# Attention and experts on one core: VectorE's row-sum work placed one piece to each gap, keys, scale and output projection placed later

## The chip, the core and the metric

The kernel runs on one core of one Trainium2 chip. The metric is device time in microseconds (us), the median of several executions; lower is better. The engines of the core work side by side and wait for one another through semaphores: TensorE (PE, with its weight loads as PEld) does matrix products, VectorE (DVE) and ScalarE (ACT) work on rows of SBUF and PSUM, GpSimd (POOL) adds here, and SyncE (SP) issues the copies.

## What is computed

A transformer block over 2048 tokens of width 128: layer norm, attention of 16 heads of width 64, layer norm, 8 experts (top 2) and a shared one. The attention, cut from the reference, is what the change touches:

```python
xq = xq.reshape(bsz, N_HEADS, seqlen, HEAD_DIM)   # a head takes 128 tokens: 2048 positions of 64
scores = jnp.einsum('bhid,bhjd->bhij', xq, xk) * SCALE
scores = jax.nn.softmax(scores, axis=-1)
out = jnp.einsum('bhij,bhjd->bhid', scores, xv)
out = out.reshape(bsz, seqlen, N_HEADS * HEAD_DIM)
return jnp.einsum('bso,ho->bsh', out, wo)
```

Each head has 2048 queries and 2048 keys; the softmax needs a maximum and a sum for each query.

## The kernel before

**Units and places.** The attention is 32 units of work, numbered 0 to 31: a head and one half of its queries each. Even units do the first half, odd ones the second. Each unit has 32 places, four to a step: at the first two TensorE computes the scores of two key tiles kt (`scores`, L1377), at the other two it weighs the values with the probabilities of the two tiles of the step before (`weigh`, L1410). After a place come the side jobs that a table hands to it (`side_jobs`, L83, from the tables at L41 to L53). Every engine runs through the same places and does its own part of each job, in that order and never out of it. A job moved to another place therefore moves on each engine that has a part in it.

**Pairs of maxima.** At each odd place stands a pair: TensorE multiplies a block of queries of a later unit with two banks of keys (`pair`, L1333, matmul at L1348) into the same two PSUM banks each time. An even pair is reduced by VectorE straight from PSUM (L1108). Of the odd ones all but pair 15 are copied out by ScalarE (`take_pair`, L894), and VectorE reduces the copy after the next odd place (`taken`, L1122); there is one copy buffer. The next pair of TensorE waits until the banks are free, so a late reduction holds up TensorE, and a late `taken` holds up ScalarE's next copy and with it the pair behind. Pair 4 stands at place 1, pair 15 at place 23, pairs 0 to 3 (of the unit after the next) at 25 to 31. After pair 15 VectorE folds the maxima together (L1112) and turns them (`peakT`, L1117).

**Shifts.** SyncE sends `peakT` on as the shifts of the next unit's scores, with eight small copies (`send_shift`, L756, issues at L764, placed at 26). TensorE's first tile of the next unit ends with a product that waits until all eight have landed (L1406).

**Keys of the next head**, in even units alone: for each of two parts TensorE projects keys (L1325); ScalarE casts them (`k_hi`) and copies them (`k_raw`); VectorE takes a difference (`step_k`, L1091); ScalarE rounds it (`round_step`, `d_hi`, L881); VectorE takes what is left (`low_k`, `d_lo`, L1099), which also frees the one bank that all projections share. SyncE then copies the halves of `k_hi`, `d_hi` and `d_lo` across (`swap_hi` L783, `swap_d` L787, issues at L780): two issues each.

**Row sums.** GpSimd adds up the probabilities in two accumulators. In the next unit VectorE turns each (`turn_sum`, L1140, a transpose of 128x1024), reduces it (`add_sum`, L1145), folds and inverts the parts (`fold_sums`, L1153). SyncE spreads the inverse to all rows through DRAM (`spread_sums`, L766), and VectorE scales the unit's output with it (`scale_unit`, L1166). In odd units from unit 3 on TensorE projects the output of the head before (`project`, L1435) and VectorE adds it to the tokens (`add_head`, L1173).

**Queue of SyncE.** SyncE is one queue: an issue that waits for a semaphore holds up all that is placed behind it.

Of the kernel before, what the change touches and what calls it, by code (L numbers as in the profile page):

```python
# [17 lines left out]
HALF = POSITIONS // 2  # L18
BANK = 512
# [19 lines left out]


LONG_JOBS = (  # L41
    {2: ("q", 0), 14: ("k", 0), 18: ("k", 1)},
    {2: ("q", 1), 6: ("v", 0), 14: ("out", 0), 19: ("v", 1)},
)
SEND_PLACE = 26

LOW_PLACES = (
    {3: ("low q", 0), 15: ("step k", 0), 16: ("low k", 0), 19: ("step k", 1), 20: ("low k", 1)},
    {3: ("low q", 1)},
)  # L50
INVERSES = 4
SUM_PLACES = {4: ("turn sum", 0), 6: ("add sum", 0), 8: ("turn sum", 1), 10: ("add sum", 1), 12: ("fold", 0)}
SCALE_PLACE, LATE_SCALE_PLACE = 20, 28  # L53

COUNTED = ("q", "k", "v")
JOBS_PER_HEAD = 6
# [26 lines left out]
def side_jobs(half, sums=True, outs=True, project=True, pairs=True, early=True, last_head=False, before_last=False):  # L83
# [21 lines left out]
    if sums:  # L105
        for place, job in SUM_PLACES.items():
            places[place].append(job)
# [10 lines left out]
def build(nc, x, wq, wk, wv, wo, gate_w, w1, w2, w3, sw1, sw2, sw3, expert_bias, cond, wmod, out):  # L118
    with ExitStack() as ctx:
        def sb(name, shape, dt=F32):  # L120
            return ctx.enter_context(nc.sbuf_tensor(name, shape, dt))

        def sem(name):
            return ctx.enter_context(nc.semaphore(name))
# [32 lines left out]
        acc = sb("acc", [P, 2, HALF])  # L157
        acc_odd = sb("acc_odd", [P, 2, HALF])
# [70 lines left out]
        added = sem("added")  # L229

        part_inverted = sem("part_inverted")
        sums_turned, sums_added, sums_inverted = sem("sums_turned"), sem("sums_added"), sem("sums_inverted")
# [33 lines left out]
        ADDS = TILES - 2  # L266
# [783 lines left out]
        def _(dve):  # L1050
# [86 lines left out]
                dve.wait_ge(o_copied, unit_done)  # L1137
                dve.tensor_tensor(oT[:, half_done, :], o_raw[:, :], job.ps, ALU.mult).then_inc(job_free, 1)

            def turn_sum(unit_done, half_done, odd):  # L1140

                dve.wait_ge(added, unit_done * ADDS + (ADDS - 1 + odd))
                dve.transpose(SumParts(unit_done).turned[odd], (acc_odd if odd else acc)[:, half_done, :]).then_inc(sums_turned, 1)

            def add_sum(unit_done, odd):  # L1145

                parts = SumParts(unit_done)
                dve.wait_ge(sums_turned, unit_done * 2 + (odd + 1))
                dve.tensor_reduce(sum_parts[:, odd * 32:odd * 32 + 32],
                                  parts.turned[odd].rearrange("p (j r) -> p j r", r=32), AX.X,  # L1150
                                  ALU.add).then_inc(sums_added, 1)
# [48 lines left out]
            def body(t):  # L1200
                local = 0
                for p, half, head, unit, plan in units(t):
                    for places in plan:
                        for jobs in places:
                            for kind, i in jobs:
# [14 lines left out]
                                if kind == "turn sum":  # L1220
                                    turn_sum(unit - 1, 1 - half, i)
                                if kind == "add sum":
                                    add_sum(unit - 1, i)
# [319 lines left out]
```

## Time and profile before

| | before |
|---|---|
| median of 3 runs (range) | 1331.19 us (1330.78 to 1331.48) |
| the profiled execution: its own time | 1330.52 us |
| its span, first to last instruction | 1328.6 us |
| granted TensorE clock, mean | 0.994 |
| busy share of the span | PE 96%, DVE 75%, ACT 67%, POOL 84% |

The share of an engine says how long it had an instruction in hand, not how long the program waited for it. TensorE's matmul ends are modelled, so that a stalled matmul can look busy: how TensorE gets on is better read from when its instructions start. A timeline row begins with its start and its length in us; a bracket at its end tells how long the engine sat idle before it and who ended that.

### The profile page before, as it was taken

How to read it: one execution, taken by the hardware profiler on the slowest of the kernel's cores; microseconds unless marked ns; L12 is line 12 of the kernel's file. 1: busy time of each engine (PE TensorE's matmuls, PEld its weight loads, DVE VectorE, ACT ScalarE, POOL GpSimd, SP SyncE). 2: the span in 40 equal slices, each digit the busy share in tenths (PEclk: the TensorE clock that was granted, in tenths of full speed). 3: DMA queues.
4: the chain of work that ended last, by engine and by line, in shares of the span. 5: the costliest groups of instructions: out<-in, count | busy, mean ns of one | idle time of the engine just before them, and what ended most of it. 6: DMA issues, size and time to landing. Idle time of an engine off the chain costs nothing. (4 is left out here: it accounts for less than half of the span.)

```text
span 1328.6 us, 22345 instructions
## 1 busy us (share of the span) xinstructions
PE 1278.2 (96%) x8604; PEld 692.3 (52%) x8604; DVE 994.6 (75%) x1253; ACT 888.4 (67%) x1096; POOL 1115.1 (84%) x507
## 2 busy tenths in 40 slices
PE   7899999999999999999999999999999999998998
PEld 5454454545554454545555454545455544444787
DVE  6677777787777777778777777787877777877575
ACT  6576667676767766676767767676767666774464
POOL 2399899898989899898989898998989898897545
PEclk9899999999999999999999999999999999998999
DMA  7020202020110202020200202020201102001423
GB/s 208 1 48 9 57 9 57 9 57 9 30 28 9 57 9 57 9 56 9 52 14 11 47 9 57 9 56 9 57 10 38 28 2 57 9 10 41 96 72 89
DMA packets 39948, 49.82 MB, mean 37 GB/s; under 512 B 8570, under 2 KB 19202, under 8 KB 39842
## 3 DMA queue, kind: packets, MB, share of 16 engines
q1 hardware_dynamic: 39698, 48.39, 14.4%
q8 instruction: 68, 1.11, 0.4%
q14 instruction: 38, 0.31, 0.1%
q10 hardware_dynamic: 144, 0.00, 0.0%
HBM read 21.83 MB, written 1.24 MB: 17 GB/s over the span
## 5 line engine op out<-in xcount | busy, mean ns | idle before, releaser
L949 ACT ACTIVATE probs<-ps 128x1024 f32<-128x1024 f32 x512 | 499.0, 1032 | 71.0 <-PE ps L1400 64.2
L1418 PE MATMUL ps<-probs,v_sb 128*64 128x512 f32 x2048 | 512.8, 607 | 0.0
L1037 POOL TENSOR_TENSOR acc<-acc,probs 128x1024 f32<-128x1024 f32 x192 | 462.8, 2410 | 49.5 <-ACT probs L949 47.3
L1108 DVE TENSOR_REDUCE peak_parts<-ps 128x2 f32<-128x1024 f32 x297 | 359.0, 1213 | 160.5 <-PE ps L1348 156.6
L1037 POOL TENSOR_TENSOR acc_odd<-acc_odd,probs 128x1024 f32<-128x1024 f32 x192 | 465.1, 2423 | 0.0
L894 ACT COPY peak_copy<-ps 128x1024 f32<-128x1024 f32 x215 | 218.6, 1017 | 257.7 <-PE ps L1348 152.8
L1122 DVE TENSOR_REDUCE peak_parts<-peak_copy 128x2 f32<-128x1024 f32 x215 | 259.9, 1209 | 34.2 <-ACT peak_copy L894 34.2
L1418 PEld LDWEIGHTS ps<-probs,v_sb 128*64 128x64 f32 x2048 | 122.1, 136 | 175.8 <-issue 139.5
L1394 PE MATMUL ps<-q_hi,d_hi 64*128 64x512 f32 x512 | 202.0, 395 | 3.8 <-ACT probs L949 3.8
L1394 PE MATMUL ps<-q_hi,d_swap_hi 64*128 64x512 f32 x512 | 201.8, 394 | 0.4 <-ACT probs L949 0.4
L1400 PE MATMUL ps<-q_hi,d_lo 64*128 64x512 f32 x512 | 201.4, 393 | 0.0
L1400 PE MATMUL ps<-q_hi,d_swap_lo 64*128 64x512 f32 x512 | 201.3, 393 | 0.0
L1397 PE MATMUL ps<-q_lo,d_hi 64*128 64x512 f32 x512 | 200.3, 391 | 0.0
L1397 PE MATMUL ps<-q_lo,d_swap_hi 64*128 64x512 f32 x512 | 200.0, 391 | 0.0
L1348 PE MATMUL ps<-k_swap_hi,q_hi 64*128 64x512 f32 x512 | 119.3, 462 | 19.5 <-DVE peak_parts L1108 14.4
L1031 POOL TENSOR_TENSOR acc_odd<-probs 128x1024 f32<-128x1024 f32 x32 | 76.7, 2397 | 68.8 <-ACT probs L949 68.8
L1348 PE MATMUL ps<-k_hi,q_hi 64*128 64x512 f32 x512 | 121.9, 472 | 11.8 <-DVE peak_parts L1108 7.6
L1348 PEld LDWEIGHTS ps<-k_swap_hi,q_hi 64*128 64x128 f32 x512 | 47.8, 184 | 148.6 <-DVE peak_parts L1108 93.6
L1348 PEld LDWEIGHTS ps<-k_hi,q_hi 64*128 64x128 f32 x512 | 48.1, 184 | 143.0 <-DVE peak_parts L1108 78.1
L1397 PEld LDWEIGHTS ps<-q_lo,d_hi 64*128 64x128 f32 x512 | 94.9, 185 | 13.6
L1394 PEld LDWEIGHTS ps<-q_hi,d_swap_hi 64*128 64x128 f32 x512 | 95.2, 186 | 10.8 <-ACT probs L949 1.3
L1394 PEld LDWEIGHTS ps<-q_hi,d_hi 64*128 64x128 f32 x512 | 95.2, 186 | 10.5 <-ACT probs L949 5.5
(244 smaller groups left out, 1573.3 us busy)
## 6 DMA issues: line engine op xcount, KB each, us to landing
k_swap_hi<-k_hi SPq DMA_DIRECT2D x64, 128.0 KB, 2.5
d_swap_hi<-d_hi SPq DMA_DIRECT2D x64, 128.0 KB, 2.3
d_swap_lo<-d_lo SPq DMA_DIRECT2D x64, 128.0 KB, 2.3
acc_odd<-sums_dram SPq DMA_DIRECT2D x62, 128.0 KB, 2.9
shifts<-peakT SPq DMA_DIRECT2D x256, 0.5 KB
q_hi<-weights_dram SPq DMA_DIRECT2D x8, 256.0 KB, 3.4
q_lo<-weights_dram SPq DMA_DIRECT2D x8, 256.0 KB, 4.9
k_hi<-weights_dram SPq DMA_DIRECT2D x8, 256.0 KB, 6.0
```

Source lines behind the costliest of these rows:

```text
L894: act.copy(peak_copy[:, :, :], ps[:, PEAK_BANK:PEAK_BANK + 2, :]).then_inc(peak_free, 1)
L949: act.activation(probs[:, kt % PROBS, :], ps[:, 2 * place:2 * place + 2, :].rearrange("p a b -> p (a b)"), ACT.Exp, scale=SCALE).then_inc( ...
L1031: pool.tensor_tensor(total, probs[:, kt, :], probs[:, kt + 1, :], ALU.add).then_inc(added, 1)
L1037: pool.tensor_tensor(total, total, probs[:, kt % PROBS, :], ALU.add).then_inc(added, 1)
L1108: dve.tensor_reduce(peak_parts[:, :, i // STRETCHES, i % STRETCHES], ps[:, bank:bank + 2, :], AX.X, ALU.max).then_inc(peak_free, 1)
L1122: dve.tensor_reduce(peak_parts[:, :, i // STRETCHES, i % STRETCHES], peak_copy[:, :, :], AX.X, ALU.max).then_inc(copy_read, 1)
L1348: mm = pe.matmul(ps[:, bank + b, :], q_hi[at, target_parity, q:q + P], keys[at, target_parity, cols], start=True, stop=True, tile_position ...
L1394: pe.matmul(ps[:, slot + b, :], hi[b][at[b], p, cols], q_hi[at[b], p, q], start=kt < 2, stop=False, tile_position=(b * HEAD_DIM, 0), skip_ ...
L1397: pe.matmul(ps[:, slot + b, :], hi[b][at[b], p, cols], q_lo[at[b], p, q], start=False, stop=False, tile_position=(b * HEAD_DIM, 0), skip_g ...
L1400: mm = pe.matmul(ps[:, slot + b, :], lo[b][at[b], p, cols], q_hi[at[b], p, q], start=False, stop=kt >= 2, tile_position=(b * HEAD_DIM, 0), ...
L1418: mm = pe.matmul(ps[at:at + HEAD_DIM, PV_BANK, :], v_sb[:, p, chunk_of(kt) * HEAD_DIM:(chunk_of(kt) + 1) * HEAD_DIM], probs[:, kt % PROBS, ...
```

## The change

In the tables the two parts of the key work go from places 14 and 18 to 18 and 22 (with their steps and lows four places later), the output projection from 14 to 22, the scale from 20 to 27 (28 to 29 in the last unit). The first sum is reduced one place later. The second accumulator is turned in two halves, at places 8 and 10, its reduction goes from 10 to 11, and the fold from 12 to 15.

```diff
 LONG_JOBS = (
-    {2: ("q", 0), 14: ("k", 0), 18: ("k", 1)},
-    {2: ("q", 1), 6: ("v", 0), 14: ("out", 0), 19: ("v", 1)},
+    {2: ("q", 0), 18: ("k", 0), 22: ("k", 1)},
+    {2: ("q", 1), 6: ("v", 0), 19: ("v", 1), 22: ("out", 0)},
 )
 LOW_PLACES = (
-    {3: ("low q", 0), 15: ("step k", 0), 16: ("low k", 0), 19: ("step k", 1), 20: ("low k", 1)},
+    {3: ("low q", 0), 19: ("step k", 0), 20: ("low k", 0), 23: ("step k", 1), 24: ("low k", 1)},
     {3: ("low q", 1)},
 )
-SUM_PLACES = {4: ("turn sum", 0), 6: ("add sum", 0), 8: ("turn sum", 1), 10: ("add sum", 1), 12: ("fold", 0)}
-SCALE_PLACE, LATE_SCALE_PLACE = 20, 28
+SUM_PLACES = {4: ("turn sum", 0), 7: ("add sum", 0), 8: ("turn sum", 1), 10: ("turn sum", 2), 11: ("add sum", 1),
+              15: ("fold", 0)}
+SCALE_PLACE, LATE_SCALE_PLACE = 27, 29
...
-            def turn_sum(unit_done, half_done, odd):
-
-                dve.wait_ge(added, unit_done * ADDS + (ADDS - 1 + odd))
-                dve.transpose(SumParts(unit_done).turned[odd], (acc_odd if odd else acc)[:, half_done, :]).then_inc(sums_turned, 1)
+            def turn_sum(unit_done, half_done, piece):
+
+                dve.wait_ge(added, unit_done * ADDS + (ADDS - 1 if piece == 0 else ADDS))
+                src, to = (acc if piece == 0 else acc_odd)[:, half_done, :], SumParts(unit_done).turned[piece > 0]
+                cols = slice(0, HALF) if piece == 0 else slice((piece - 1) * BANK, piece * BANK)
+                dve.transpose(to[:, cols], src[:, cols]).then_inc(sums_turned, 1)
...
-                dve.wait_ge(sums_turned, unit_done * 2 + (odd + 1))
+                dve.wait_ge(sums_turned, unit_done * 3 + (3 if odd else 1))
```

The new lines push all that stands below them down by up to three lines, so L1348 before is L1351 in the changed kernel.

What the tables do is seen in the engines' order. On VectorE, in the middle of a unit, from the reduction of the first sum (`sum_parts<-k_raw`) on; before:

```order
L1149 TENSOR_REDUCE sum_parts<-k_raw 128x32 [waits sums_turned]
L1143 STREAM_TRANSPOSE acc<-acc_odd 128x1024 [waits added]
L1108 TENSOR_REDUCE peak_parts<-ps 128x2 [waits peak_full]
L1122 TENSOR_REDUCE peak_parts<-peak_copy 128x2 [waits peak_free]
L1149 TENSOR_REDUCE sum_parts<-acc 128x32 [waits sums_turned]
L1157 STREAM_TRANSPOSE acc_odd<-sum_parts 128x64 [waits sums_added]
L1159 TENSOR_REDUCE acc_odd<-acc_odd 32x32 [waits dve_chain]
L1159 TENSOR_REDUCE acc_odd<-acc_odd 32x32 x3
L1163 TENSOR_REDUCE acc_odd<-acc_odd 32x32 [waits dve_chain]
L1164 RECIPROCAL acc_odd<-acc_odd 32x32 [waits dve_chain]
L1108 TENSOR_REDUCE peak_parts<-ps 128x2 [waits peak_full]
L1122 TENSOR_REDUCE peak_parts<-peak_copy 128x2 [waits peak_free]
```

and in the changed kernel:

```order
L1152 TENSOR_REDUCE sum_parts<-k_raw 128x32 [waits sums_turned]
L1146 STREAM_TRANSPOSE acc<-acc_odd 128x512 [waits added]
L1109 TENSOR_REDUCE peak_parts<-ps 128x2 [waits peak_full]
L1123 TENSOR_REDUCE peak_parts<-peak_copy 128x2 [waits peak_free]
L1146 STREAM_TRANSPOSE acc<-acc_odd 128x512 [waits added]
L1152 TENSOR_REDUCE sum_parts<-acc 128x32 [waits sums_turned]
L1109 TENSOR_REDUCE peak_parts<-ps 128x2 [waits peak_full]
L1123 TENSOR_REDUCE peak_parts<-peak_copy 128x2 [waits peak_free]
L1160 STREAM_TRANSPOSE acc_odd<-sum_parts 128x64 [waits sums_added]
```

One half of the transpose now stands behind pair 8 and the copy of pair 7, and the fold, which begins with the 128x64 transpose, behind pair 10 and the copy of pair 9 instead of ahead of them.

On VectorE at the end of an even unit, from the second part of the keys (`ps<-ps,k_raw` is the step, `d_lo` the low) or from pair 14 to pair 0; before:

```order
L1091 TENSOR_TENSOR ps<-ps,k_raw 128x512 [waits raw_ready]
L1099 TENSOR_TENSOR d_lo<-ps,d_hi 128x512 [waits d_hi_ready]
L1170 TENSOR_TENSOR oT<-o_raw,acc_odd 128x512 [waits o_copied,sums_spread]
L1108 TENSOR_REDUCE peak_parts<-ps 128x2 [waits peak_full]
L1122 TENSOR_REDUCE peak_parts<-peak_copy 128x2 [waits peak_free]
L1108 TENSOR_REDUCE peak_parts<-ps 128x2 [waits peak_full]
L1112 TENSOR_REDUCE peak<-peak_parts 128x8 [waits peak_free]
L1117 STREAM_TRANSPOSE peakT<-peak 128x32 [waits shift_ready,peak_ready]
L1108 TENSOR_REDUCE peak_parts<-ps 128x2 [waits peak_ready,peak_full]
```

and in the changed kernel:

```order
L1109 TENSOR_REDUCE peak_parts<-ps 128x2 [waits peak_full]
L1123 TENSOR_REDUCE peak_parts<-peak_copy 128x2 [waits peak_free]
L1109 TENSOR_REDUCE peak_parts<-ps 128x2 [waits peak_full]
L1113 TENSOR_REDUCE peak<-peak_parts 128x8 [waits peak_free]
L1118 STREAM_TRANSPOSE peakT<-peak 128x32 [waits shift_ready,peak_ready]
L1092 TENSOR_TENSOR ps<-ps,k_raw 128x512 [waits raw_ready]
L1100 TENSOR_TENSOR d_lo<-ps,d_hi 128x512 [waits d_hi_ready]
L1109 TENSOR_REDUCE peak_parts<-ps 128x2 [waits peak_ready,peak_full]
L1173 TENSOR_TENSOR oT<-o_raw,acc_odd 128x512 [waits o_copied,sums_spread]
```

The step and the low of the second part of the keys, which stood ahead of pair 14, now stand behind the turning of the maxima and ahead of pair 0; the scale stands behind pair 0.

SyncE's order is the same in both kernels. This is its end of an even unit in the changed one:

```order
L781 DMA d_swap_hi<-d_hi 64x512 [waits d_hi_ready]
L781 DMA d_swap_hi<-d_hi 64x512
L781 DMA d_swap_lo<-d_lo 64x512 [waits job_free]
L781 DMA d_swap_lo<-d_lo 64x512
L765 DMA shifts<-peakT 1x4x32 [waits peak_turned]
L765 DMA shifts<-peakT 1x4x32 x7
```

The copies of the second part of the keys stood ahead of the eight shifts before, too; what these copies wait for now comes later on VectorE and ScalarE.

## Rows read from the trace of the kernel before

**Rows 1.** The whole run's waits: who waited for whom; us in total, times, longest.

```profile
ACT peak_copy L894 <- DVE peak_parts L1122: 104.7, 92, 2.4
```

**Rows 2.** Timeline of PE, end of unit 16: pairs 9 to 12, 14 to 2, then shifts.

```profile
648.64 0.50 PE L1348 MATMUL ps<-k_hi,q_hi 64*128 64x512 f32 x2
650.86 0.51 PE L1348 MATMUL ps<-k_swap_hi,q_hi 64*128 64x512 f32 x2 [0.34 <-ACT peak_copy L894]
...
654.03 0.50 PE L1348 MATMUL ps<-k_swap_hi,q_hi 64*128 64x512 f32 x2
...
656.16 0.51 PE L1348 MATMUL ps<-k_hi,q_hi 64*128 64x512 f32 x2 [0.22 <-ACT peak_copy L894]
...
661.07 0.40 PE L1348 MATMUL ps<-k_swap_hi,q_hi 64*128 64x512 f32 x2
...
664.06 0.50 PE L1348 MATMUL ps<-k_swap_hi,q_hi 64*128 64x512 f32 x2 [0.72 <-DVE peak_parts L1108]
666.32 0.50 PE L1348 MATMUL ps<-k_hi,q_hi 64*128 64x512 f32 x2 [0.35 <-DVE peak_parts L1108]
...
668.62 0.50 PE L1348 MATMUL ps<-k_hi,q_hi 64*128 64x512 f32 x2
...
670.34 0.40 PE L1348 MATMUL ps<-k_swap_hi,q_hi 64*128 64x512 f32 x2
...
673.57 0.40 PE L1406 MATMUL ps<-shifts,minus 64*128 64x512 f32 x2
```

**Rows 3.** Timeline of ACT in unit 16: copy of pair 9, a rounding, copy of pair 1.

```profile
649.79 1.02 ACT L894 COPY peak_copy<-ps 128x1024 f32<-128x1024 f32 x1 [1.66 <-DVE peak_parts L1122]
...
660.79 0.59 ACT L881 CAST d_hi<-ps 128x512 fp32r<-128x512 f32 x1
...
669.16 1.02 ACT L894 COPY peak_copy<-ps 128x1024 f32<-128x1024 f32 x1 [1.90 <-PE ps L1348]
```

**Rows 4.** Timeline of DVE in unit 16: transposes, second key part, pair 15 to pair 0.

```profile
646.23 1.23 DVE L1143 STREAM_TRANSPOSE acc<-acc_odd 128x1024 f32<-128x1024 f32 x1
...
650.86 0.25 DVE L1157 STREAM_TRANSPOSE acc_odd<-sum_parts 128x64 f32<-128x64 f32 x1
...
659.70 0.70 DVE L1091 TENSOR_TENSOR ps<-ps,k_raw 128x512 f32<-128x512 f32 x1
661.42 0.69 DVE L1099 TENSOR_TENSOR d_lo<-ps,d_hi 128x512 fp32r<-128x512 f32 x1 [1.02 <-ACT d_hi L881]
...
665.05 1.21 DVE L1108 TENSOR_REDUCE peak_parts<-ps 128x2 f32<-128x1024 f32 x1
...
666.52 0.21 DVE L1117 STREAM_TRANSPOSE peakT<-peak 128x32 f32<-128x32 f32 x1
666.86 1.23 DVE L1108 TENSOR_REDUCE peak_parts<-ps 128x2 f32<-128x1024 f32 x1
```

**Rows 5.** Timeline of SP, end of unit 16: issues of the second key part and shifts.

```profile
661.41 1.10 SPq L780 DMA_DIRECT2D d_swap_hi<-d_hi  x2
662.55 1.24 SPq L780 DMA_DIRECT2D d_swap_lo<-d_lo  x2
666.76 5.01 SPq L764 DMA_DIRECT2D shifts<-peakT  x8
```

**Rows 6.** Timeline of SP ahead of unit 0: issues of the first shifts.

```profile
42.76 5.01 SPq L764 DMA_DIRECT2D shifts<-peakT  x8
```

**Rows 7.** Timeline of PE, start of unit 0: the product that waits for these.

```profile
48.81 0.80 PE L1406 MATMUL ps<-shifts,minus 64*128 64x512 f32 x2 [1.77 <-DMA shifts<-peakT]
```

**Rows 8.** Timeline of PE, pairs with waits: unit 0, two of unit 29, unit 30.

```profile
77.62 0.50 PE L1348 MATMUL ps<-k_hi,q_hi 64*128 64x512 f32 x2 [0.38 <-DVE peak_parts L1108]
...
1144.72 0.50 PE L1348 MATMUL ps<-k_swap_hi,q_hi 64*128 64x512 f32 x2 [1.43 <-DVE peak_parts L1108]
...
1148.15 0.50 PE L1348 MATMUL ps<-k_hi,q_hi 64*128 64x512 f32 x2 [1.54 <-DVE peak_parts L1108]
...
1172.12 0.51 PE L1348 MATMUL ps<-k_swap_hi,q_hi 64*128 64x512 f32 x2 [0.72 <-DVE peak_parts L1108]
```

## The prediction

> **What bounds the kernel now.** TensorE has the most work, so I ask first what holds it up. The list of the run's waits names ScalarE's copies of pairs, which waited 104.7 us in all for VectorE to reduce the copy before [rows 1]. What that costs TensorE is read from starts, since its ends are modelled: in the timeline of unit 16 I take the distance from one pair to the next, and compare distances that hold the same work. From pair 1 to pair 2 (two score tiles, nothing late) it is 670.34 - 668.62 = 1.72 us. From pair 9 to pair 10, the same work, it is 2.22, and from pair 11 to pair 12 it is 2.13: 0.50 and 0.41 lost, both with ScalarE's copy named in the bracket [rows 2]. ScalarE's own row says why: the copy of pair 9 waited for VectorE's `taken` [rows 3], and that stood behind the first sum and a whole transpose. From pair 0 to pair 1 (two weighings) it is 2.30, from pair 14 to pair 15, the same work, 2.99: 0.69 lost to VectorE [rows 2], where the low of the second key part and the scale stand ahead of pair 14's reduction. Pair 0 comes 2.26 behind pair 15 where 1.72 would do: 0.54 more.
>
> The other thing to see is what must be done when a unit ends. The turned maxima are ready at 666.52 + 0.21 = 666.73 [rows 4], SyncE begins to send the shifts at 666.76 [rows 5], and TensorE uses them at 673.57 [rows 2], 6.81 after the first issue. What the sending needs is seen once, ahead of unit 0, where TensorE really waited for it: from the first issue at 42.76 [rows 6] to the product at 48.81 [rows 7] it is 6.05. So unit 16 has 0.76 us to spare, and no more.
>
> **The change part by part.** All figures are for an ordinary even unit, of which there are 14 (2 to 28).
>
> *Row sums, one piece to a gap.* A whole transpose takes 1.23 and one of 64 columns 0.25 [rows 4], which makes some 0.18 plus 1.02 ns a column: a half is about 0.71 (an estimate), two halves 1.43, 0.2 more than the whole. It buys that 0.5 less stands ahead of the `taken` on which pair 9's copy waits, where 0.50 were lost, and that the whole fold stands behind the `taken` on which pair 11's copy waits, where 0.41 were lost. The dear bound for a half is the whole 1.23: then the first `taken` gains nothing. The cheap one is half of 1.23. I take 0.71, nearest to the two rows that it is drawn from. The copies would then end just as TensorE wants the banks.
>
> *Second key part, and scale, away from pair 14.* The 0.69 goes. Also the reduction of pair 15 began 665.05 - 664.06 = 0.99 after its product [rows 2, 4], since VectorE was still busy; a free engine begins 669.16 - 668.62 = 0.54 after [rows 2, 3]. That is 0.45 more. In all the turned maxima come 0.50 + 0.41 + 0.69 + 0.45 = 2.05 sooner in the unit; I take 2.0, with 1.14 (only the last two) and 2.4 (the short delays of a pair after each wait as well) as bounds.
>
> *What stands behind the turned maxima now.* Step and low of the second key part come after them on VectorE, and SyncE has the copies of that part ahead of the shifts. This is the part that I think decides. The next instruction on VectorE began 666.86 - 666.73 = 0.13 after the turning, a step takes 0.70 [rows 4], I give 0.05 to the hand-over, the rounding on ScalarE takes 0.59 [rows 3], SyncE took it up 661.41 - 661.38 = 0.03 later [rows 3, 5], the four issues ran from 661.41 to 663.79, which is 2.38 [rows 5], and 0.05 go by before the next. Together 3.93 from turned maxima to the first shift issue, where it was 0.03: 3.90 later. The low (0.69) ends inside the first two issues and adds nothing. Bounds: 3.7 without the small gaps; 4.1 if the four issues keep the pace of the last two (1.24 each two, with gaps).
>
> So the shifts are 3.90 - 2.0 = 1.9 later in the unit than before, 0.76 of that was to spare, and the next unit begins **1.14 us** later.
>
> By the Trainium skill, page "DMA: Bandwidth & Descriptors", section "Anatomy of one DMA — SWDGE (gpsimd) path", a copy has a fixed cost of about 2.0 us, most of it the receipt after the last byte. These copies are issued by SyncE, not GpSimd; eight issues in 5.01 put the last one 4.38 after the first, so [rows 6, 7] leave 1.67 for it. By the page's figure an even unit would lose 0.33 more, some 5 us in the run; the measured pair of rows is taken.
>
> *A new wait inside the unit that costs nothing more.* Pair 0's reduction now stands behind step, rounding and low: 0.13 + 0.70 + 0.05 + 0.59 + 0.03 + 0.69 = 2.19 after the turned maxima, ending 3.42 after. TensorE wants to issue pair 1 some 666.32 + 2.30 - 666.73 = 1.89 after them [rows 2], so it waits 1.5 there. ScalarE's exponentials of two tiles also stand behind that rounding. But the end of the unit is set by the shifts, later still, so this wait lies inside the 1.14.
>
> *Moves at no cost.* The first key part goes through the same four places of spacing as the second did. The scale waits for nothing new and lies in the time in which VectorE waits for pair 2; without that cover it would cost its second or less to pair 2. The output projection is the same TensorE work eight places later in odd units; VectorE's addition now waits for it between pairs 14 and 15, but pair 15's product is issued behind the projection anyway. SyncE's eight shifts there have no key copies ahead, and keep their slack. I put odd units at 0, give or take 0.1.
>
> *The units that differ.* Unit 0 has no row sums, and its only VectorE wait of note is 0.38 at pair 0 [rows 8]: it loses 3.90 - 0.45 - 0.76 = 2.7. Unit 29 carries the statistics of the second layer norm in the same gaps as the scale, and TensorE waited 1.43 and 1.54 there [rows 8]; with scale and projection moved I let 2.7 of that go. Unit 30 has no keys: its wait of 0.72 [rows 8] goes, and with the copies' share I take 1.0. Unit 31, the start and the experts: 0.
>
> **Sum.** 14 x 1.14 = 16.0, + 2.7 - 2.7 - 1.0 = 15.0 us. The profiled execution took 1330.5, which gives 1345.5; the median of the runs stands 0.7 above it, so **1346 us**.
>
> **Rivals.**
> *Shifts are not the end of the unit (faster).* If SyncE's send came early enough, TensorE would keep its gains: 0.50 + 0.41 + 0.69 and the 0.54 at pair 0, less the new 1.5 at pair 1, that is -0.6 in 14 units, +1.1 in unit 0, -3.7 in units 29 and 30: 11 less, 1320 us. It decides at 0.76 + 2.0 = 2.8 us: if less than that lies between the turned maxima and the first shift issue. My chain has 3.93, and its largest piece, four issues on one queue, is read directly; for this rival over a quarter of it would have to overlap. By the Trainium skill, the same page and section, waits for semaphores are taken by the issuing sequencer before dispatch, which leaves no room for the shifts to pass the key copies; that SyncE's issues never overlap in these rows agrees. Chance 0.11.
> *Gain and delay cancel.* If the gaps give 2.4 and the chain takes 3.7, an even unit loses 0.54, the run 14 x 0.54 - 1.0 = 6.6: 1338. For no change that can be told, a little more would have to go well (1333). Chance of that 0.07.
> *The halves cost like wholes (slower still).* Then pairs 10 and 12 keep their waits, the maxima come only 1.14 sooner and an even unit loses 2.0: 14 x 2.0 - 1.0 = 27, 1359 us. Against it speaks that a small transpose is five times shorter [rows 4]. Chance 0.08.
> The forecast itself, with its bounds, 0.74.
>
> **How the numbers follow.** About 0.2%, 2.7 us, is what a measurement of this kernel can tell from no change. Slower takes the forecast and the last rival, 0.82; the same 0.07; faster 0.11. The range runs from 1334, just below the case in which most goes well, to 1358, just below the last rival; it leaves out the faster rival and the far end of the slower one, under 2 in 10.
>
> **What would show it.** In an even unit of the changed kernel: pair 9 to 10 and 11 to 12 near 1.75, pair 14 to 15 without a wait (and longer by the key projection); the turned maxima 2.0 sooner in the unit; SyncE's first shift issue about 3.9 behind them; a wait at pair 1 for VectorE; and a wait of TensorE at the shift product (L1409 there) of each odd unit for the shifts, 1.0 to 2.0 us long. If that last wait is missing, the forecast is wrong and the first rival holds. If it is there and the pairs 10 and 12 still wait, the third holds.

## The result and the profile after

| | before | after |
|---|---|---|
| median (range) | 1330.99 us (1325.78 to 1331.48, 4 runs) | 1366.22 us (1363.61 to 1378.64, 4 runs) |
| ratio, 95% interval | | 1.0292 [1.0225, 1.036] |
| profiled execution, span | 1330.52, 1328.6 us | 1378.64, 1376.6 us |
| granted TensorE clock, mean | 0.994 | 0.985 |

Slower, as forecast, but by 35 us where 15 were forecast, and 8 us beyond the range. The four runs of the changed kernel lie 15 us apart. The profiled one, the slowest, has four units with a long stall that is shown below; by the price of one such unit, worked out further down, the other three runs would have had two to three each (an estimate, since they have no trace).

**What came as forecast.** Unit 16 again. TensorE's pairs 9 to 12, 14, 15, 0 to 3 and the first shift product of the next unit, from the timeline of PE after (start and length in us; the bracket is the idle time before and who ended it):

```profile
681.77 0.50 PE L1351 MATMUL ps<-k_hi,q_hi 64*128 64x512 f32 x2
683.52 0.51 PE L1351 MATMUL ps<-k_swap_hi,q_hi 64*128 64x512 f32 x2
685.82 0.50 PE L1351 MATMUL ps<-k_swap_hi,q_hi 64*128 64x512 f32 x2
687.65 0.50 PE L1351 MATMUL ps<-k_hi,q_hi 64*128 64x512 f32 x2
...
692.52 0.42 PE L1351 MATMUL ps<-k_swap_hi,q_hi 64*128 64x512 f32 x2
...
695.61 0.50 PE L1351 MATMUL ps<-k_swap_hi,q_hi 64*128 64x512 f32 x2
697.43 0.50 PE L1351 MATMUL ps<-k_hi,q_hi 64*128 64x512 f32 x2
700.96 0.49 PE L1351 MATMUL ps<-k_hi,q_hi 64*128 64x512 f32 x2 [1.17 <-DVE peak_parts L1109]
702.66 0.41 PE L1351 MATMUL ps<-k_swap_hi,q_hi 64*128 64x512 f32 x2
704.87 0.50 PE L1351 MATMUL ps<-k_swap_hi,q_hi 64*128 64x512 f32 x2
707.68 0.50 PE L1409 MATMUL ps<-shifts,minus 64*128 64x512 f32 x2 [1.61 <-DMA shifts<-peakT]
```

From pair 9 to 10 it is 1.75 now and from 11 to 12 it is 1.83, where [rows 2] had 2.22 and 2.13. Pair 15 and pair 0 come without a wait. Pair 1 waits 1.17 for VectorE, and the shift product waits 1.61 for the shifts. VectorE's half transpose, turning, step, low, pair 0 and scale in the same unit, from its timeline:

```profile
682.28 0.70 DVE L1146 STREAM_TRANSPOSE acc<-acc_odd 128x512 f32<-128x512 f32 x1
...
697.63 0.21 DVE L1118 STREAM_TRANSPOSE peakT<-peak 128x32 f32<-128x32 f32 x1
697.77 0.67 DVE L1092 TENSOR_TENSOR ps<-ps,k_raw 128x512 f32<-128x512 f32 x1
699.08 0.69 DVE L1100 TENSOR_TENSOR d_lo<-ps,d_hi 128x512 fp32r<-128x512 f32 x1 [0.65 <-ACT d_hi L882]
699.69 1.22 DVE L1109 TENSOR_REDUCE peak_parts<-ps 128x2 f32<-128x1024 f32 x1
700.82 2.16 DVE L1173 TENSOR_TENSOR oT<-o_raw,acc_odd 128x512 f32<-128x512 f32 x1
```

and SyncE's queue behind the turning, from the timeline of SP:

```profile
699.08 1.10 SPq L781 DMA_DIRECT2D d_swap_hi<-d_hi  x2
700.22 1.31 SPq L781 DMA_DIRECT2D d_swap_lo<-d_lo  x2
701.58 5.02 SPq L765 DMA_DIRECT2D shifts<-peakT  x8
```

The turned maxima are ready at 697.63 + 0.21 = 697.84, and the first shift leaves at 701.58, 3.74 later (0.03 in [rows 4, 5]). The product comes 6.10 after that, where the prediction took 6.05 from [rows 6, 7]. Unit 16, from shift product to shift product, takes 38.10 (before 37.11). The last row of VectorE's timeline already holds the surprise: the scale takes 2.16.

**What was not forecast.** The waits of TensorE and ScalarE in the whole run (us in total, times, longest), from the list of waits after:

```profile
ACT peak_copy L895 <- DVE peak_parts L1123: 148.5, 107, 7.4
PE ps L1351 <- DVE peak_parts L1109: 43.1, 27, 5.6
PE ps L1409 <- DMA shifts<-peakT: 26.3, 16, 2.6
```

The third row is the forecast wait. The first was 104.7 with a longest of 2.4 [rows 1] and was to shrink; it grew, and 7.4 is a length that nothing in the prediction makes. The group of the scale says where the long ones come from (shortest, median and longest in ns), before

```profile
L1170 DVE TENSOR_TENSOR oT<-o_raw,acc_odd x31: 691/890/2207, 107.7 to 1221.7; 128x512 f32<-128x512 f32 x31
```

and after:

```profile
L1173 DVE TENSOR_TENSOR oT<-o_raw,acc_odd x31: 693/2152/9017, 116.6 to 1269.9; 128x512 f32<-128x512 f32 x31
```

The same instruction on the same data takes up to 9.0 us. Unit 5 is one of four odd units (5, 9, 11, 27) in which it does. VectorE there, timeline after, pair 0 to pair 2:

```profile
265.17 1.23 DVE L1109 TENSOR_REDUCE peak_parts<-ps 128x2 f32<-128x1024 f32 x1
266.31 9.02 DVE L1173 TENSOR_TENSOR oT<-o_raw,acc_odd 128x512 f32<-128x512 f32 x1
275.25 1.21 DVE L1109 TENSOR_REDUCE peak_parts<-ps 128x2 f32<-128x1024 f32 x1
```

GpSimd in the same stretch, the 11th to the 14th add of the unit and the first of the next:

```profile
265.42 2.40 POOL L1038 TENSOR_TENSOR acc<-acc,probs 128x1024 f32<-128x1024 f32 x1
267.74 2.43 POOL L1038 TENSOR_TENSOR acc_odd<-acc_odd,probs 128x1024 f32<-128x1024 f32 x1
270.08 2.40 POOL L1038 TENSOR_TENSOR acc<-acc,probs 128x1024 f32<-128x1024 f32 x1
272.38 2.39 POOL L1038 TENSOR_TENSOR acc_odd<-acc_odd,probs 128x1024 f32<-128x1024 f32 x1
281.87 2.35 POOL L1032 TENSOR_TENSOR acc<-probs 128x1024 f32<-128x1024 f32 x1 [7.09 <-ACT probs L950]
```

TensorE, pairs 2 and 3:

```profile
268.64 0.40 PE L1351 MATMUL ps<-k_swap_hi,q_hi 64*128 64x512 f32 x2
...
276.51 0.79 PE L1351 MATMUL ps<-k_swap_hi,q_hi 64*128 64x512 f32 x2 [5.60 <-DVE peak_parts L1109]
277.11 0.62 PE L1397 MATMUL ps<-q_hi,d_hi 64*128 64x512 f32 x1
```

and each engine's busy time by stretch, with the granted clock in the third column from the right:

```profile
268.00:274.00 6.00, 2.91 (x18) 1.00 (x14) 6.00 (x1) 2.31 (x3) 6.00 (x3) 1.00 0.00 0
274.00:276.00 2.00, 0.00 (x0) 0.00 (x0) 2.00 (x2) 0.00 (x0) 0.77 (x1) 0.80 0.00 0
276.00:282.00 6.00, 5.49 (x24) 3.43 (x26) 3.62 (x4) 3.26 (x4) 0.14 (x1) 0.50 0.01 1
282.00:290.00 8.00, 8.00 (x64) 4.41 (x60) 5.83 (x7) 5.06 (x7) 3.98 (x2) 1.00 0.01 2
```

Read together: the scale began inside the 11th add and ended at 275.33, 0.56 after the 14th had ended (274.77) and GpSimd had nothing ready any more. (In the program the first add of the next unit waits for this scale, `out_scaled`, so only the unit's own adds can go ahead of it.) Four adds ran at their usual 2.4 while it stood. Pair 2's reduction waited behind it, so TensorE sat idle for 5.60, and then went on at the lower of its two clock levels (0.50, which is 1.2 GHz; a score product takes 0.62 instead of 0.39) until 282. Unit 5 took 43.37 where its undisturbed neighbours take 36.85, and the units behind the four took 38.9 to 39.9 instead of 38.0.

### The profile page after: what moved, and what is told of

The parts are those of the page before. It is cut to its first block and busy times, and to the rows that moved or that the text cites. A ratio compares the mean times of both kernels' runs of the same rounds, so it can differ in the third digit from the quotient of the medians.

```text
span 1376.6 us, 22362 instructions
## 1 busy us (share of the span) xinstructions
PE 1289.4 (94%) x8604; PEld 696.2 (51%) x8604; DVE 1059.2 (77%) x1284; ACT 890.5 (65%) x1096; POOL 1113.6 (81%) x507
## 5 line engine op out<-in xcount | busy, mean ns | idle before, releaser
L1038 POOL TENSOR_TENSOR acc_odd<-acc_odd,probs 128x1024 f32<-128x1024 f32 x192 | 470.1, 2448 | 0.0
L895 ACT COPY peak_copy<-ps 128x1024 f32<-128x1024 f32 x215 | 218.5, 1016 | 240.7 <-DVE peak_parts L1123 148.5
L1351 PE MATMUL ps<-k_swap_hi,q_hi 64*128 64x512 f32 x512 | 120.2, 465 | 25.2 <-DVE peak_parts L1109 25.1
L1351 PE MATMUL ps<-k_hi,q_hi 64*128 64x512 f32 x512 | 124.2, 481 | 18.1 <-DVE peak_parts L1109 18.0
L1032 POOL TENSOR_TENSOR acc<-probs 128x1024 f32<-128x1024 f32 x32 | 76.4, 2387 | 62.1 <-ACT probs L950 62.1
L1351 PEld LDWEIGHTS ps<-k_hi,q_hi 64*128 64x128 f32 x512 | 48.4, 186 | 152.4 <-DVE peak_parts L1109 82.2
L1351 PEld LDWEIGHTS ps<-k_swap_hi,q_hi 64*128 64x128 f32 x512 | 48.1, 184 | 151.8 <-DVE peak_parts L1109 92.5
L1403 PEld LDWEIGHTS ps<-q_hi,d_lo 64*128 64x128 f32 x512 | 95.7, 187 | 11.7
```

What stands on the lines that cost most here:

```text
L895: act.copy(peak_copy[:, :, :], ps[:, PEAK_BANK:PEAK_BANK + 2, :]).then_inc(peak_free, 1)
L1032: pool.tensor_tensor(total, probs[:, kt, :], probs[:, kt + 1, :], ALU.add).then_inc(added, 1)
L1038: pool.tensor_tensor(total, total, probs[:, kt % PROBS, :], ALU.add).then_inc(added, 1)
L1351: mm = pe.matmul(ps[:, bank + b, :], q_hi[at, target_parity, q:q + P], keys[at, target_parity, cols], start=True, stop=True, tile_position ...
L1403: mm = pe.matmul(ps[:, slot + b, :], lo[b][at[b], p, cols], q_hi[at[b], p, q], start=False, stop=kt >= 2, tile_position=(b * HEAD_DIM, 0), ...
```

## The experiments

**Is it the scale's place beside GpSimd's adds, and only that?** Theory: VectorE and GpSimd can't both have two operands out of SBUF at once, so VectorE's scale (both operands in SBUF) stands until the adds let it in. Rival: the whole is a matter of the shifts' queue, or of the scale standing at 27 as such. Four kernels. (The letters of theories and rivals here and below are those of the expectations.)

*One operand of the scale from PSUM*, nothing else changed:

```diff
-                dve.tensor_tensor(oT[:, half_done, :], o_raw[:, :], SumParts(unit_done).spread,
+                dve.tensor_tensor(oT[:, half_done, :], o_raw[:, :], ps[:, JOB_BANK, :],
```

> The changed kernel with one operand swapped: the scale multiplies o_raw with a bank of PSUM instead of the spread inverse in SBUF (so the scaling by the row sums is left out; the waits stay). Theory A (a scale with two SBUF operands is kept waiting by GpSimd's adds, from about 2.1 us to 9.0 us, and the 9.0 ones in odd units stop TensorE for 5.6 us and halve its clock for some 7 us): every scale takes about 0.7 us, no odd unit is longer than about 36.9 us, and the run comes to 1345 us plus or minus 4, which is my forecast for the rest. Rival B (the 9 us are a wait of VectorE for something else at that place, a copy of the sums or a semaphore): the long ones stay and the run stays near 1366 or above.

Measured 1347.34 us (1345.87 to 1348.13), ratio to before 1.0138 [1.0116, 1.0159]. The group of the scale in this kernel:

```profile
L1173 DVE TENSOR_TENSOR oT<-o_raw,ps x31: 646/676/686, 116.8 to 1238.6; 128x512 f32<-128x512 f32 x31
```

No scale is longer than 0.69, every one of them beside the same adds; TensorE's wait for the shifts stays (25.6 us, 16 times). So the long scales need the second operand in SBUF, they are worth 1366.2 - 1347.3 = 19 us in the median run, and without them the time is near the forecast of 1346, in part by luck, as is shown below. ScalarE's copies still wait 123.3 us in this kernel (107 times, longest 1.3): of the 148.5 above, the scale made the long ones, and the rest of the growth from 104.7 belongs to the other moves.

*SyncE sends the shifts ahead of the last d copies:*

```diff
-                                    swap_d(head * 2 + (3 + i), Job(jobs_at(t) + (local - 1)), i, 1 - p)
+                                    held = (head * 2 + (3 + i), Job(jobs_at(t) + (local - 1)), i, 1 - p)
+                                    if i == 0:
+                                        swap_d(*held)
...
+                                    if held:
+                                        swap_d(*held)
+                                        held = None
```

> The changed kernel with SyncE's copies of the second key part's d issued behind the eight shifts instead of ahead of them. Theory A (even units end with the shifts, which stand behind those copies): the wait of 1.66 us at the shift product of 15 odd units goes, even units come to about 36.3 us, the run is some 25 us below the changed kernel if the long scales stay as many, so about 1341 us, and the wait at pair 1 stays at 1.2 us. Rival B (even units are held by the wait at pair 1 and the late exponentials, not by the queue of SyncE): the wait moves elsewhere and less than 8 us are won.

Measured 1385.24 us (1375.44 to 1397.82), ratio 1.0406 [1.0334, 1.0478]. The queue did what was meant. SP and TensorE in unit 16 of this kernel, from the timelines (the maxima were turned at 699.07):

```profile
699.10 5.01 SPq L765 DMA_DIRECT2D shifts<-peakT  x8
704.16 1.17 SPq L781 DMA_DIRECT2D d_swap_hi<-d_hi  x2
```

```profile
706.11 0.49 PE L1356 MATMUL ps<-k_swap_hi,q_hi 64*128 64x512 f32 x2
707.14 0.39 PE L1414 MATMUL ps<-shifts,minus 64*128 64x512 f32 x2
```

The wait for the shifts is gone and an undisturbed even unit takes 36.35 instead of 38.0. So the queue costs 1.65 in each even unit, and without it such a unit is shorter than before's 37.11. But eight odd units had a long scale instead of four, and the run came out slower. The two costs have different causes; one was cured, and the other, left to itself, ate the gain.

*Only the scale moved, everything else as before:*

```diff
-SCALE_PLACE, LATE_SCALE_PLACE = 20, 28
+SCALE_PLACE, LATE_SCALE_PLACE = 27, 29
```

> The kernel before with the scale alone moved, from place 20 to 27 (29 in the last unit). Theory A (place 27 is a bad one beside GpSimd's adds): the scale takes 1.4 us or more in most units instead of 0.85 to 1.04, and if it falls into an add as in the changed kernel some odd units lose 6 to 7 us each, with a halved clock behind them; even units gain up to 0.8 us each at pair 15, so 1320 us without any long scale and 1335 to 1360 with some. Rival B (as I had forecast, the scale is free at 27): it takes about 1 us everywhere and the run comes to 1318 to 1324 us.

Measured 1317.66 us (1317.01 to 1318.03), ratio 0.9915 [0.9895, 0.9935]: faster than before. Its scales take 0.88 in odd units and 2.75 in even ones, none more. So place 27 alone isn't the trouble, and moving the scale away from pair 14 is a gain.

*Changed kernel with the keys back at 14 and 18:*

```diff
-    {2: ("q", 0), 18: ("k", 0), 22: ("k", 1)},
+    {2: ("q", 0), 14: ("k", 0), 18: ("k", 1)},
...
-    {3: ("low q", 0), 19: ("step k", 0), 20: ("low k", 0), 23: ("step k", 1), 24: ("low k", 1)},
+    {3: ("low q", 0), 15: ("step k", 0), 16: ("low k", 0), 19: ("step k", 1), 20: ("low k", 1)},
```

> The changed kernel with the keys back at places 14 and 18, their steps and lows at 15, 16, 19 and 20; row sums, scale and output projection stay as changed. Theory A (keys behind the turned maxima cost the even units 1.66 us at the shifts; the scale costs the odd ones): no TensorE wait for shifts and none at pair 1 in even units, which come to about 36 us with a wait near pairs 10 to 13 where fold and first key part now share a gap; long scales may stay. Without them 1318 us, with four of them about 1350. Rival B (the row-sum order itself makes the units longer): even units stay at 37.5 us or more.

Measured 1355.51, 1353.81, 1343.04 and 1313.25 us, four runs of one kernel. In the profiled one (1355.51) five odd units had a long scale and took 43.2 to 43.3; undisturbed even units take 35.95, odd ones 36.75. Five at some 7.8 us each (the price worked out below) are 39 of the 42 us between this run and the fastest, which therefore seems to have had none; it has no trace. So long scales come with the keys at their old places too.

**Does the moment at which the scale meets the add decide?** In the long cases the scale began some 0.9 into the 11th add of the unit, in the harmless odd units of the version with the scale alone 2.03 into the 10th. Two kernels shift only that, with a reduction on VectorE ahead of the odd units' scale whose result nobody reads. In the changed kernel, to get out of that moment:

```diff
+                                if kind == "scale" and half == 1 and unit < UNITS - 1:
+                                    dve.tensor_reduce(sum_parts[:, 0:32], k_raw[:, P:P + 512].rearrange(
+                                        "p (j r) -> p j r", r=16), AX.X, ALU.add)
```

> The changed kernel with one idle reduction of 512 columns (about 0.65 us, result unused) ahead of the scale on VectorE in odd units but the last. In the changed kernel every odd scale begins 0.85 to 0.93 us into one of GpSimd's adds, and some of those, and no others, are kept waiting 9.0 us. Theory A1 (the long wait comes only from that moment of the add): the scale now begins about 1.5 us into an add, takes about 1.5 us, none is long, and the run comes to 1345 us plus or minus 4. Rival C (any scale ahead of three queued adds can be kept out until GpSimd pauses, whatever the moment): long scales stay, and the run stays above 1355 us.

Measured 1373.63 us (1354.55 to 1399.89). The scales began 1.48 into the add, and two of the profiled run were long all the same, 8.4. In the version with the scale alone, to get into that moment (the same reduction, with 1024 columns):

> The scale alone at place 27 (1317.7 us, odd scales beginning 2.03 us into an add and taking 0.88), with an idle reduction of 1024 columns (1.13 us) ahead of the odd scales. Theory A1: the odd scales now begin about 0.85 us into the next add; some of them take 9.0 us, TensorE loses about 6.7 us for each and more behind it through the halved clock, and the run comes to 1330 to 1370 us and varies from execution to execution. Rival D (the long waits need the changed order of row sums or the late output projection, and the moment is a bystander): no scale takes more than 3 us and the run stays at 1318 us plus or minus 3.

Measured 1318.33 us (1315.24 to 1319.88), ratio 0.9906 [0.9878, 0.9934]. The scales began 0.84 into the 11th add, took 2.1, and none was long. So that moment is not needed for a long scale, and alone it does not bring one: the moment is refuted as the cause.

**Which of the moves brings them?** *Changed kernel with keys and projection back* (the keys' lines as above):

```diff
-    {2: ("q", 1), 6: ("v", 0), 19: ("v", 1), 22: ("out", 0)},
+    {2: ("q", 1), 6: ("v", 0), 14: ("out", 0), 19: ("v", 1)},
```

> The changed kernel with keys and output projection back at their old places: of the change, only the row sums one to a gap and the scale at 27 are left. Theory A: even units as with the keys back (35.9 us), no shift wait. The odd scales leave the bad moment, since the odd unit's TensorE work ahead of the scale is again that of the kernel with the scale alone moved (there 2.03 us into an add): no long scale, and 1308 to 1314 us, below the 1317.7 of the scale alone. Rival E (the row-sum order itself brings the odd scale to the bad moment): long scales stay, and the run varies between 1313 and 1356 us as with the keys back alone.

Measured 1313.39 us (1313.08 to 1314.48), ratio 0.9873 [0.9849, 0.9897]: this beats both kernels. Its scale:

```profile
L1173 DVE TENSOR_TENSOR oT<-o_raw,acc_odd x31: 691/1473/2757, 114.1 to 1203.9; 128x512 f32<-128x512 f32 x31
```

Even units take some 35.95, odd ones 36.5, and no scale is long. *The same with the second transpose whole again, at place 8:*

```diff
-SUM_PLACES = {4: ("turn sum", 0), 7: ("add sum", 0), 8: ("turn sum", 1), 10: ("turn sum", 2), 11: ("add sum", 1),
+SUM_PLACES = {4: ("turn sum", 0), 7: ("add sum", 0), 8: ("turn sum", 1), 11: ("add sum", 1),
```

> As the run with keys and output projection back, but the second accumulator turned whole at place 8. Theory A (the halves free pair 10, the fold's place pair 12): in even units the distance from pair 9 to pair 10 is again 2.2 us instead of about 1.75, pair 11 to 12 stays near 1.8, even units come to about 36.4 us, and the run is 5 to 8 us above the one with halves if neither has long scales. Rival F (the halves buy nothing): the two agree within 2 us.

Measured 1318.66 us (1314.84 to 1330.3, 10 runs), ratio 0.9927 [0.99, 0.9954]: the halves are worth some 5 us, about 0.45 in each even unit (36.4 against 35.95), as the prediction's 0.50 for pair 10 said. No scale is long in its trace. Two of its ten runs, 1327.6 and 1330.3, lie 7 to 10 us above the next; they have no trace, so a long scale in them can't be excluded.

*Changed kernel with only the projection back* (the diff of the projection's line alone):

> The changed kernel with only the output projection put back from place 22 to 14; keys, row sums and scale stay as changed. Theory E (the projection at 22 is what lets odd units' scales fall into the stretch in which GpSimd's adds shut them out; the keys have no part in it): no scale over 3 us, odd units 36.5 to 36.9, even ones 38.0 with their wait of 1.6 for the shifts, 1340 to 1348 us, all runs within 4 us. Theory K (the moved keys matter as much): scales of some 9 us in at least two odd units, runs 8 us or more apart, median 1350 or more.

Measured 1346.33 us (1343.08 to 1346.65), ratio 1.0137 [1.0115, 1.0159]. No scale over 2.2; even units 38.0 with their wait of 1.65 for the shifts, odd ones 36.66. Theory E: with the projection at 14 none of five kernels had a long scale in its profile, with it at 22 all four that keep the scale on VectorE, with SBUF operands and nothing held back, had some. That is one traced execution of each kernel, some 14 odd units in each. The moved keys alone don't bring long scales (this kernel), and the keys at their old places don't keep them out (the kernel above with the keys back at 14 and 18).

**Do the following adds keep the scale out?** GpSimd holds the 12th add of odd units until the scale is done:

```diff
                     for n in range(1, ADDS + 1):
+                        if n == 12 and half == 1 and unit < UNITS - 1:
+                            pool.wait_ge(out_scaled, unit)
                         add(unit, half, n)
```

> The changed kernel in which GpSimd waits for the scale ahead of its 12th add of every odd unit but the last. Theory A (a waiting scale is passed over by one GpSimd add after the other as long as the next one is ready): with the next add held, every odd scale ends with the add that it meets, at 0.7 to 3.0 us, no pair waits over 2 us, odd units 36.6 to 37.2, no stretch at granted clock 0.50 in them, 1343 to 1350 us with runs within 4 us. Theory F (it isn't the following adds that hold the scale, the first one alone or something else does): scales of over 5 us stay in some odd units and 1355 us or more, or the held add delays the exponentials and odd units take 38 us or more throughout.

Measured 1347.64 us (1346.91 to 1348.96), ratio 1.0147 [1.0128, 1.0167]. The scale of unit 5 in VectorE's timeline of this kernel, and the adds around the scales of units 1 (the first two rows) and 5 in GpSimd's:

```profile
266.31 2.05 DVE L1175 TENSOR_TENSOR oT<-o_raw,acc_odd 128x512 f32<-128x512 f32 x1
```

```profile
116.83 2.40 POOL L1038 TENSOR_TENSOR acc<-acc,probs 128x1024 f32<-128x1024 f32 x1
119.87 2.38 POOL L1038 TENSOR_TENSOR acc_odd<-acc_odd,probs 128x1024 f32<-128x1024 f32 x1 [0.63 <-DVE oT L1175]
...
265.44 2.37 POOL L1038 TENSOR_TENSOR acc<-acc,probs 128x1024 f32<-128x1024 f32 x1
268.43 2.36 POOL L1038 TENSOR_TENSOR acc_odd<-acc_odd,probs 128x1024 f32<-128x1024 f32 x1 [0.62 <-DVE oT L1175]
```

The scale of unit 5 starts at the same 266.31, into the same add, and takes 2.05 instead of 9.02; the only difference is that the next add waits 0.62 for it. All ordinary odd units are alike (2.03 to 2.06). Theory A holds, and unit 1 shows it once more, beyond its bound of 3.0: there the scale met the 10th add, was passed over by the 11th, and came in where the 12th (119.87) was held, after 3.82. One odd unit (25) took 38.38 with a short scale, and in it the expectation of no stretch at the lower clock failed: the unit begins with a wait of 2.06 for the shifts (1.47 two units earlier), and the granted clock of its first 4 us was 0.57. Unit 25 is as long in the changed kernel (38.47) and with the scale from PSUM (38.44), so this isn't the scale's doing.

**Both costs away**, the shifts first and the add held:

> The changed kernel with both costs taken away: SyncE sends the shifts ahead of the last d copies, and GpSimd's 12th add of odd units waits for the scale. Theory (the two costs are all that made the change slow, and they add): even units 36.3 to 36.6 with no wait for shifts, odd 36.6 to 37.2 with no long scale, 1315 to 1325 us. Rival (without one cost the other grows, as in the version with shifts first, where more scales were long): still 1335 us or more.

Measured 1319.91 us (1318.99 to 1320.76), ratio 0.9937 [0.9918, 0.9956]. Even units 36.35 without a wait for shifts, odd ones 36.73. With both costs away the kernel is faster than before, so these two made the change slow. It stays some 6.5 us above the version with keys and projection back, whose even units take 35.95.

**A candidate**: in the fastest version, GpSimd does the scale behind its 11th add.

```diff
+                        if n == 11 and 0 < unit < UNITS - 1:
+                            pool.wait_ge(sums_spread, 32 * unit)
+                            pool.wait_ge(o_copied, unit)
+                            pool.tensor_tensor(oT[:, 1 - half, :], o_raw[:, :], SumParts(unit - 1).spread,
+                                               ALU.mult).then_inc(out_scaled, 1)
```

> The version with row sums in pieces and scale at 27 but keys and projection where they were, with the scale done by GpSimd behind its 11th add instead of by VectorE (the last unit keeps VectorE's). Theory A (in that version VectorE's scale of 2.75 in even units is a wait for GpSimd and costs a part of it at pair 2): even units 0.3 to 0.8 shorter, 1302 to 1310 us. Rival G (that wait lies under cover, or GpSimd's scale delays its adds and with them the exponentials): 1311 to 1325 us.

Measured 1315.40 us (1314.38 to 1318.14, 6 runs), ratio 0.9906 [0.9888, 0.9924]. Rival G: GpSimd takes 1.29 for it, VectorE's 2.75 is gone, and even units stay at 35.95. That wait lay under cover. It gains nothing in time over 1313.4, though it takes the scale out of the contest between the two engines (all but the last unit's).

## Why the prediction was wrong, and where it was right

- *Row sums, one piece to a gap* (pairs 10 and 12): right. A half takes 0.70 (forecast 0.71), the pairs come after 1.75 and 1.83.
- *Turned maxima 2.0 sooner*: right. In unit 16 they come 697.84 - 669.58 = 28.26 after the unit's first shift product, before 666.73 - 636.46 = 30.27: 2.01.
- *Shifts behind the second key part, 3.93*: it was 3.74. The step began at 697.77, before the recorded end of the turning at 697.84, where 0.13 after it was taken; the four issues ran 2.45 (forecast 2.38). The way from first issue to product was 6.10 against 6.05 by [rows 6, 7], so the rows were right for SyncE's copies. By the 2.0 us that the Trainium skill's page "DMA: Bandwidth & Descriptors", section "Anatomy of one DMA — SWDGE (gpsimd) path", gives for GpSimd's copies, it would have been 6.38 (an estimate from the page's figure).
- *Even unit +1.14*: +0.89. The mechanism was right, the size 0.25 too large, most of it the 3.93. The first rival falls: the shifts are the end of the unit. So does the second, since the gaps gave 2.0 and not 2.4, and the third: the halves don't cost like wholes. (The third rival's own sum, 27 on top of 1331.2, makes 1358 and not 1359.)
- *Wait at pair 1 inside the unit, 1.5*: there, 1.17, and hidden.
- *Units 0, 29, 30*: +2.47, -1.6, -0.94 (forecast +2.7, -2.7, -1.0).
- *Odd units at 0, give or take 0.1*: +0.33 in the ordinary ones, and 0.14 with the projection back at 14: moving the projection wasn't free. (Unit 1, which has no projection, came 1.0 shorter, and unit 25 1.9 longer, see above.) Without long scales the odd units 1 to 27 cost 4.7 us together, and that offset what the even units fell short, 12.6 where 16.0 were forecast. That the kernel without long scales comes within 1.3 us of the forecast is luck to this extent.
- **The step that failed** is, under *Moves at no cost*: "The scale waits for nothing new and lies in the time in which VectorE waits for pair 2; without that cover it would cost its second or less to pair 2." It waits for no new semaphore, but, once begun, for GpSimd: 2.05 to 2.16 in most units, 9.0 in some odd ones. The cover beside pair 2 is 2.12 long in odd units and 1.62 in even ones (VectorE's idle time at that place with the scale from PSUM, which takes 0.68 itself), so the short ones cost nothing and the long ones come out as 5.6 of stall and then a stretch at half clock. Each costs about (1378.6 - 1347.3) / 4 = 7.8 us; the profiled run had four. Without them, by the units of the version with the scale from PSUM, it is 12.6 in the even units 2 to 28, 4.7 in the odd ones, 2.5 in unit 0, -2.1 in unit 29 and -0.9 in unit 30: 16.8 over 1330.5 gives 1347.3; the profiled execution of that kernel took 1348.1, the median of its runs is 1347.3.
- Where the trace of before could have warned: the scale there took from 0.69 to 2.21, the first in unit 31, where GpSimd was idle. An instruction that takes three times as long on the same shape may depend on a neighbour, and moving it moves it to another neighbour. The prediction took the duration as its own. The Trainium skill has the rule, on the page "SBUF — State Buffer", section "Who interferes with whom": a VectorE instruction with two inputs in SBUF contends with a GpSimd instruction that reads SBUF, and the loser is blocked fully. The scales of 0.68 with one input from PSUM agree. A scale kept out over four adds goes beyond the one instruction that a reader would take from it.

Two things stay open: what passes a waiting scale over in some units and lets it in after one add in others, and why scales of 8 us and more were traced only with the projection at place 22. The moment within the add isn't it. Nor is it a next add that isn't ready yet: what the 12th add needs was there 1.84 before the end of the 11th in unit 5 of the changed kernel, where the scale took 9.02, and 1.83 before it in unit 7, where it took 2.06. And a projection in the same unit isn't needed: unit 1 has none, and its scale was passed over once with the 12th add held (3.82).

## What to carry to other kernels

Before moving a VectorE instruction with two SBUF operands, look at its shortest and longest duration in the trace: if they differ, price it by what GpSimd has ready at the new place, and let GpSimd wait for it, give it to GpSimd, or take one operand from PSUM (run here only with the scaling by the row sums left out). Ask of every move what the one queue behind it holds: here eight small copies, due at the end of the unit, stood behind four that nobody needed yet. And when four runs of one kernel spread by 1%, look for an instruction whose longest duration is a multiple of its median before explaining the median.

## What the runs showed of the hardware

- A VectorE multiplication of 128x512 with both operands in SBUF took 0.69 alone, and beside GpSimd's adds ended some 0.55 after the end of an add, not always the first: 2.05, 3.82 and 9.02 were seen. With one operand from PSUM it took 0.68 beside the same adds.
- GpSimd lost little: the add behind a scale that got in took 2.8 instead of 2.4.
- After 5.60 without a product TensorE went on at a granted clock of 0.50 for some 6 us, so that the stall was paid for again in part.
